# Local attention: half of a tile's columns shifted by one token, by two DMA transfers or by a shift matrix

## The reference, cut to what matters

```python
def shift_token(t):
    t1, t2 = jnp.split(t, 2, axis=-1)
    t2 = jnp.pad(t2, ((0, 0), (1, 0), (0, 0)))[:, :-1]
    return jnp.concatenate([t1, t2], axis=-1)

def _layer(x, wqkv, qs, ksc, wo, lg, lb, w1, b1, w2, b2):
    h = shift_token(x)
    ...                                   # q, k, v, rotary, attention in windows of 64 tokens
    x = x + o @ wo
    h = shift_token(x)
    mu = h.mean(-1, keepdims=True)
    var = h.var(-1, keepdims=True)
    h = (h - mu) / jnp.sqrt(var + 1e-05) * lg + lb
    h = h @ w1 + b1
    a, g = jnp.split(h, 2, axis=-1)
    h = a * jax.nn.gelu(g, approximate=False)
    x = x + h @ w2 + b2
```

## Time and profile before

| | |
|---|---|
| runs, not profiled: median (lowest, highest) | 1104.02 us (1098.06, 1105.16) |
| the profiled execution | 1102.0 us |
| its span, first to last instruction | 1100.2 us |
| mean granted TensorE clock | 0.899 of full speed |
| the four instances of `window_layer`, about | us 85 to 180, 192 to 290, 639 to 727, 743 to 838 |

### The profile page before, as it was taken

The page is one execution under the profiler, slowest core; times in us unless marked ns, Lnnn a source line. Parts: engine busy times, 40 slices in busy tenths (PEclk is TensorE's granted clock), DMA queues, the critical chain, the costliest instruction groups (busy, mean ns, idle before and its releaser), DMA issues.

```text
span 1100.2 us, 18999 instructions
## 1 busy us (share of the span) xinstructions
PE 881.5 (80%) x6776; PEld 536.6 (49%) x6776; DVE 665.9 (61%) x1736; ACT 491.6 (45%) x1010; POOL 468.4 (43%) x485
## 2 busy tenths in 40 slices
PE   6767998799836888999387679987988378889993
PEld 3544766377523444444245547754765234444442
DVE  5887885687576655311268688756875766543113
ACT  4114763676334653531041257636763346635310
POOL 4677871586411422200165778616864114222001
PEclk9998999999967896999789889899999669959997
DMA  9001100110000000000100011001100000000001
GB/s 364 31 2 30 26 16 1 30 26 17 1 0 1 1 1 1 1 1 1 39 2 1 1 30 26 16 1 30 26 16 1 0 1 1 1 1 1 1 1 38
DMA packets 11630, 21.62 MB, mean 20 GB/s; under 512 B 1424, under 2 KB 6928, under 8 KB 11024
## 3 DMA queue, kind: packets, MB, share of 16 engines
q1 hardware_dynamic: 11248, 18.60, 5.8%
q10 hardware_dynamic: 288, 1.78, 0.4%
HBM read 11.87 MB, written 1.05 MB: 12 GB/s over the span
## 4 chain that ended last, share of the span: by engine, by line
PE 48%; DVE 28%; POOL 9%; issue 6%; ACT 4%; DMA 1%; POOLq 1%; SPq 0%; DVEq 0%; ACTq 0%
PE bank L798 10%; PE bank L368 9%; PE bank L719 4%; DVE arena L1161 4%; PE bank L788 3%; PE bank L487 2%; DVE arena L859 2%; DVE arena L915 2%; DVE arena L1020 2%; PE bank L705 2%; PE bank L616 2%; POOL arena L1641 2%; PE bank L686 2%; POOL arena L1649 2%; PE bank L561 2%
## 5 line engine op out<-in xcount | busy, mean ns | idle before, releaser
L368 PE MATMUL bank<-consts_sb,arena 128*128 128x128 f32 x1024 | 160.5, 300 | 98.9 <-DVE arena L1153 26.2
L1290 ACT ACTIVATE arena<-bank 128x512 f32<-128x512 f32 (+2 forms) x300 | 146.4, 556 | 155.9 <-PE bank L368 93.6
L368 PEld LDWEIGHTS bank<-consts_sb,arena 128*128 128x128 f32 x1024 | 124.7, 152 | 170.0 <-issue 75.4
L1568 POOL TENSOR_TENSOR rstd<-vareps,neghalf 128x1 f32<-128x1 f32 x96 | 53.4, 558 | 254.5 <-DVE vareps L854 253.0
L1161 DVE TENSOR_REDUCE arena<-bank 128x2 f32<-128x1024 f32 (+3 forms) x128 | 98.1, 818 | 81.1 <-PE bank L673 80.5
L1697 POOL TENSOR_SCALAR_AFFINE_SELECT arena<-arena 128x256 f32<-128x256 f32 x128 | 51.3, 414 | 202.3 <-ACT arena L1481 199.4
L1641 POOL TENSOR_TENSOR arena<-arena,neghalf 128x16 f32<-128x16 f32 x32 | 93.1, 2908 | 66.0 <-DVE arena L1022 65.8
L487 PE MATMUL bank<-weights,x_features 128*128 128x512 f32 x192 | 102.1, 650 | 15.0 <-DVE arena L1035 9.2
L798 PE MATMUL bank<-arena,weights 128*128 128x512 f32 x256 | 111.9, 594 | 1.6 <-ACT arena L1537 1.6
L1481 ACT ACTIVATE arena<-bank 128x1024 f32<-128x1024 f32 (+1 forms) x96 | 81.5, 881 | 37.0 <-PE bank L705 36.6
L1408 ACT ACTIVATE arena<-bank,arena 128x128 f32<-128x128 f32 x256 | 69.7, 383 | 50.1 <-DVE arena L1063 50.1
(11 more groups left out here) (167 smaller groups left out, 1641.2 us busy)
## 6 DMA issues: line engine op xcount, KB each, us to landing
arena<-arena SPq DMA_DIRECT2D x56, 130.0 KB, 2.3
weights<-wts_dram SPq DMA_DIRECT2D x1, 2824.0 KB, 19.3
weights<-wts_dram SPq DMA_DIRECT2D x1, 1817.0 KB, 13.3
weights<-wts_dram SPq DMA_DIRECT2D x1, 1561.0 KB, 9.4
x_tokens<-x_dram SPq DMA_DIRECT2D x6, 256.0 KB, 3.2
consts_sb<-consts_dram ACTq DMA_DIRECT2D x1, 1226.5 KB, 7.2
out_dram<-x_inner SPq DMA_DIRECT2D x16, 64.0 KB, 1.5
consts_sb<-consts_dram SPq DMA_DIRECT2D x1, 768.0 KB, 4.7
```

The lines of the kernel that those rows point to most:

```text
L368: mm = pe.transpose(bank[:, i * P:(i + 1) * P], src, ident)
L1290: return act.activation(dst, src, ACT.Copy)
```

## The change

The shift of tile g is made by SP with two transfers inside SBUF: rows 0 to 126 of `xi[:, g, 64:128]` to rows 1 to 127 of `hn2`, and one row (the last token of the tile before, or zeros for the first tile of a sequence, taken from row 0 of the constant `carry`) to row 0. SP's loop gets G + 3 steps; after the value transfers of tile s it does `one_later(l, s - 3)`, which waits for xa_ready of tile s-3 and, from the third tile of all on, for PE's transpose of the tile two before it, since that used the same `hn2` buffer. DVE waits for hs_landed where it waited for pe_hs, and its copy and the wait for itself behind it are gone; its wait for pe_hT moves to `shifted_normed`. PE's two products, their PSUM bank use, the constant `shift` and POOL's wait for pe_hs are gone.

```diff
@@ window_layer, PE
-                    g = s - 4
-                    if 0 <= g < G:
-                        n = G * l + g
-                        pe.wait_ge(xa_ready, n + 1)
-                        bank = take(pe, ("hs", n), [(hs_kept, n + 1)], bank=BANK2["hs"])
-                        mm = pe.matmul(bank[:, 0:64], c_("shift"), xi[:, g, 64:P], start=True, stop=(g % NT == 0))
-                        if g % NT:
-                            mm = pe.matmul(bank[:, 0:64], c_("carry"), xi[:, g - 1, 64:P], start=False, stop=True)
-                        mm.then_inc(pe_hs, 1)
@@ window_layer, DVE
                 def shifted_stats(g):
                     n = G * l + g
-                    dve.wait_ge(pe_hs, n + 1)
+                    dve.wait_ge(hs_landed, 32 * (n + 1))
+                    dve.wait_ge(xa_ready, n + 1)
+                    norm_stats(first + g, [xi[:, g, 0:64], hn2[:, g % 2, 64:P]])
+
+                def shifted_normed(g):
+                    n = G * l + g
                     if n >= 2:
                         dve.wait_ge(pe_hT, hn_seen(n - 2))
-                    dve.tensor_copy(hn2[:, g % 2, 64:P], held(("hs", n))[:, 0:64]).then_inc(hs_kept, 1)
-                    dve.wait_ge(hs_kept, n + 1)
-                    dve.wait_ge(xa_ready, n + 1)
-                    norm_stats(first + g, [xi[:, g, 0:64], hn2[:, g % 2, 64:P]])
-
-                def shifted_normed(g):
                     norm_apply(first + g, hn2[:, g % 2, 0:64], xi[:, g, 0:64])
                     norm_apply(first + g, hn2[:, g % 2, 64:P], hn2[:, g % 2, 64:P]).then_inc(hn_ready, 1)
@@ gelu_layer, POOL
-                pool.wait_ge(pe_hs, G * (l + 1))
@@ SP
+            def one_later(l, g):
+                n = G * l + g
+                sp.wait_ge(xa_ready, n + 1)
+                if n >= 2:
+                    sp.wait_ge(pe_hT, hn_seen(n - 2))
+                ahead = xi[P - 1:P, g - 1, 64:P] if g % NT else c_("carry")[0:1, 0:64]
+                sp.dma_start(hn2[1:P, g % 2, 64:P], xi[0:P - 1, g, 64:P]).then_inc(hs_landed, 16)
+                sp.dma_start(hn2[0:1, g % 2, 64:P], ahead).then_inc(hs_landed, 16)
...
-                    for g in range(G):
+                    for s in range(G + 3):
+                        if s < G:
...
+                        if s >= 3:
+                            one_later(l, s - 3)
```

More of the change, by code:

```diff
@@ L57 @@
      ("rot2", NT * 4 * D2),
-     ("shift", 128), ("carry", 128)])
+     ("carry", 128)])
 MASKS_WIDTH = P
@@ L235, in build @@
          rot_ready, q_rotated, q_ready, pe_qT, pe_kT, qT_ready, kk_ready, vA_ready, pe_S, shift_ready, P_ready, pe_PT,
-         PT2_ready, pe_O, o_ready, pe_oT, oT_ready, pe_wo2, xa_ready, pe_hs, hs_kept, hn_ready, pe_wg, pe_wa, gel_ready,
+         PT2_ready, pe_O, o_ready, pe_oT, oT_ready, pe_wo2, xa_ready, hs_landed, hn_ready, pe_wg, pe_wa, gel_ready,
          hh_ready, xb2_ready, pe_w2, xf_ready) = (counter(n) for n in (
@@ L240, in build @@
              "pe_S", "shift_ready", "P_ready", "pe_PT", "PT2_ready", "pe_O", "o_ready", "pe_oT",
-             "oT_ready", "pe_wo2", "xa_ready", "pe_hs", "hs_kept", "hn_ready", "pe_wg", "pe_wa", "gel_ready", "hh_ready",
+             "oT_ready", "pe_wo2", "xa_ready", "hs_landed", "hn_ready", "pe_wg", "pe_wa", "gel_ready", "hh_ready",
              "xb2_ready", "pe_w2", "xf_ready"))
@@ L352, in build @@
         CENTRED1 = 6
-        BANK2 = {"hT": 3, "q": 0, "k": 1, "v": 2, "hs": 3, "qT": 4, "kT": 5, "oT": 3, "PT": (6, 2), "S": (4, 5),
+        BANK2 = {"hT": 3, "q": 0, "k": 1, "v": 2, "qT": 4, "kT": 5, "oT": 3, "PT": (6, 2), "S": (4, 5),
                  "wo2": 3, "O": (6, 2)}
@@ L993, in shifted_stats @@
                     n = G * l + g
-                    dve.wait_ge(pe_hs, n + 1)
-                    if n >= 2:
-                        dve.wait_ge(pe_hT, hn_seen(n - 2))
-                    dve.tensor_copy(hn2[:, g % 2, 64:P], held(("hs", n))[:, 0:64]).then_inc(hs_kept, 1)
-                    dve.wait_ge(hs_kept, n + 1)
+                    dve.wait_ge(hs_landed, 32 * (n + 1))
                     dve.wait_ge(xa_ready, n + 1)
@@ L1002, in shifted_normed @@
                 def shifted_normed(g):
+                    n = G * l + g
+                    if n >= 2:
+                        dve.wait_ge(pe_hT, hn_seen(n - 2))
                     norm_apply(first + g, hn2[:, g % 2, 0:64], xi[:, g, 0:64])
@@ L1748, in _ @@
                 for l in range(2):
-                    for g in range(G):
[L1750 to L1759, removed]
+                    for s in range(G + 3):
+                        if s < G:
+                            g = s
+                            n = G * l + g
+                            sp.wait_ge(vA_ready, n + 1)
+                            if n >= 4:
+                                sp.wait_ge(pe_O, 2 * (n - 3))
+                            sp.dma_start(vS2[64:P, n % 4, :, :], vA2[0:64, n % 4, :, :]).then_inc(vS_landed[n % 4], 16)
+                            if g % NT < NT - 1:
+                                if n >= 3:
+                                    sp.wait_ge(pe_O, 2 * (n - 2))
+                                sp.dma_start(vS2[0:64, (n + 1) % 4, :, :], vA2[64:P, n % 4, :, :])\
+                                    .then_inc(vS_landed[(n + 1) % 4], 16)
+                        if s >= 3:
+                            one_later(l, s - 3)
                 for g in range(G):
@@ L1864, in _layout @@
     later = np.where(i[None, :] > i[:, None], -1e30, 0.0)
-    c["shift"] = i[None, :] == i[:, None] + 1
     c["carry"] = (i[:, None] == P - 1) & (i[None, :] == 0)
```

## The result

The changed kernel takes 1133.76 us (median of six, 1132.91 to 1138.50), the kernel before, run beside it, 1102.3 us (1098.06 to 1105.16): a ratio of 1.0301 (95% interval 1.0279 to 1.0322). The forecast was 1158 in a range of 1108 to 1245, so sign and range hold, and the loss is 31.5 us instead of 56. The profiled execution spans 1132.4 us against 1100.2.

What follows compares the result with a forecast made beforehand. No engine has slack, so DVE's in-order wait for the shift closes a loop: 12.9 us in each of four instances, 52 us, plus 4 for the clock, on 1102.0 gives 1158 us, range 1108 to 1245.

Steps and rivals of the forecast that it cites:

- steps 1, 2 and 4 of the sum: DVE's shifted statistics start 2.0 us late, 8.0 by step 7 in a closed loop of 11.2 us steps, 12.9 after the drain.
- D(4): Start of DVE's shifted statistics in step 4, forecast 2.0 us late; the number in brackets is the step.
- L: Time from the shift's trigger until DVE may start its statistics: 5.0 us forecast, each us worth 28 us of time.
- One engine for 127 rows: 127 is prime, so one DMA engine carries the shift's rows, at 28.5 ns a packet; chance 0.70 at an ordinary pace.
- step 3: Step 8 of the kernel: PE's L627 ends an unchanged 17.66 us after step 7's statistics start; the next start is 11.8 late.
- step 6: Lower granted clock around the drain, some widening matmuls at the lower level: 1 us an instance, 4 us in all.
- xa(3): End of DVE's L1069 in step 3, making the rows that the next step shifts; the number in brackets is the step.
- (a) to (c): Removed: PE's L507 and L509, some 13 us; DVE's copy L997, 7 us at most; PE's wait for that copy, 7.3 us.
- (d): The drain's wait of DVE for the last shift, 2.33 us, is replaced, not removed.
- Sixteen engines: Rival: the shift's rows spread unevenly over sixteen engines, landing in 2.1 to 2.9 us, time about 1097 us; chance 0.12.
- Slow packets: Rival: one engine, but 60 ns per 256-byte packet, so a latency of 9.0 us and 1270 us; chance 0.10.
- The lower clock in the main steps: Rival: PE's gaps lower its clock, L627 becomes the trigger, steps of 12.5 us, 1180 us; chance 0.08.

Runs made afterwards that it cites:

- e5: Changed kernel with the 127-row transfer issued a second time into unused space and waited for too: 1195.7 us, ratio 1.0854 to the kernel before.
- e3: Changed kernel with DVE's shifted statistics moved later in steps 4 to 7, behind the maxima, transfers unchanged: 1113.3 us, ratio 1.0098 to the kernel before.
- e1: Changed kernel with one transfer of all 128 rows in place of 127 + 1, leaving out the shift: 1092.6 us, ratio 0.9913 to the kernel before.
- e8: Changed kernel with 128 unshifted rows, then a single row into unused space, both waited for: 1091.0 us in one execution.
- e2: Changed kernel with the 127 rows split into 112 + 15, so three transfers with the single row: 1107.6 us, ratio 1.0049 to the kernel before.
- e4: Changed kernel without transfer or wait for the shift, statistics and normalisation reading unshifted columns: 1087.2 us, ratio 0.9863 to the kernel before.

## Why the prediction was right, and where its sizes were off

**What bounds, and the closed loop (steps 1, 2 and 4 of the sum): right.** The first late moment is D(4), the main steps are DVE's 6.17 us plus L, the drain steps 1.15 plus L, in every instance. e5 gives 29 us per us of L where 28 were foreseen; e3 takes the cost away without touching the transfer, by moving what waits for it. The threshold was put at about L = 3.1, from steps of 9.2 us. Without PE's products and DVE's copy the steps are shorter: 8.99 us in e1 (D(5) = 237.70, D(8) = 264.67, no wait for the shift in them), and 8.99 - 6.17 gives about 2.8. That agrees with e1 and e8 (L 1.8 and 2.3: no loop) and with e2 (L 3.2 to 3.7: steps of 9.4 to 9.9).

**One engine for 127 rows: right.** e1, e8 and e2 show it. The Trainium skill ("DMA: Bandwidth & Descriptors", section on why a DMA increments its semaphore by 16 and not by 1) had given one engine for 127 partitions, and by that rule the traces agree, with shares of 0.08 against 0.77. What I had read from the trace before, that the transfers with equal shares each leave sixteen small packets, was a sound sign too, but my own test with it was wrong. The packets of the SP queue rose by 16368 - 11248 = 5120, and 5120 = 4096 + 1024 is what I had written down for sixteen engines. My count of packets for each transfer was off. The queue's rows of e1 and of e5:
```profile
q1 hardware_dynamic: 15856, 19.58, 6.2%
q1 hardware_dynamic: 20464, 20.62, 6.1%
```
e1 adds 4608 = 32 x (128 + 16) to the kernel before: an even transfer has sixteen end packets. e5 adds 4096 = 32 x (127 + 1) to the changed kernel: a transfer of 127 rows has one. The changed kernel's 160 a tile are then 127 + 1 for the 127 rows and 32 for the single row, which I had taken for one data packet. The sizes in the trace say the same: 4064 packets of 256 bytes, 512 of 16 bytes, and 544 = 32 x 17 ends of 4 bytes. So the single row goes as sixteen pieces of 16 bytes with sixteen ends, and the end packets do tell how many engines carry a transfer, if each transfer is counted by itself.

**The size of L: the term that was mis-sized.** I took 28.5 ns a packet from 512-byte packets to DRAM, so 3.6 us for 127, and 1.4 us for the rest. Measured: 14.1 ns and 1.8 us for the packets, 2.1 us for the rest, L = 3.93 and not 5.0. The packets cost half of what I took, nearer to the size scaled by bytes (17.6 ns, L = 3.6). The fixed part was too small by 0.8 us: it is 1.5 already in e1, the landing of the 127 rows is slower than that of an even transfer by 0.28 us and their start by 0.14, and the second transfer hides but for 0.18 us. These are two errors of opposite sign, 1.8 us too much and 0.8 too little; that they cancelled in part is luck. Read with L = 3.93, the prediction's slope takes 28 x 1.07 = 30 us off 1158 and leaves 1128, 6 us under the 1133.8 measured.

**The threshold on PE (step 3) and the clock (step 6): the first roughly right, the second too small.** In the second instance D(7) to the end of L618 in step 8 was to stay at 17.66 us. PE's timeline, steps 5 and 8 (counterpart of the earlier trace rows), and steps 8, 9 and 10 in the table of stretches (counterpart of the earlier trace rows):
```profile
256.05 0.33 PE L618 MATMUL bank<-consts_sb,arena 128*128 128x128 f32 x1
...
280.76 3.67 PE L368 MATMUL bank<-consts_sb,arena 128*128 128x128 f32 x16 [1.69 <-POOL arena L1644]
...
289.06 0.33 PE L618 MATMUL bank<-consts_sb,arena 128*128 128x128 f32 x1
```
```profile
280.00:291.00 11.00, 9.60 (x100) 8.16 (x101) 3.87 (x13) 5.53 (x14) 1.26 (x2) 0.70 0.01 2
293.30:298.30 5.00, 2.54 (x25) 2.08 (x20) 2.49 (x11) 1.88 (x2) 0.55 (x1) 0.85 0.05 10
298.30:303.30 5.00, 4.69 (x10) 2.14 (x10) 1.55 (x7) 0.69 (x1) 0.54 (x1) 0.50 0.03 7
```
289.39 - 270.65 = 18.7 us, 1.1 more, in a stretch whose granted clock is 0.70 (0.84 before). In step 10 it is 0.50, the lower level of 1.2 GHz throughout: PE had been busy for 2.5 of 5.0 us in step 9. From xa(3) to D(11) the four instances grew by 8.9, 6.3, 5.9 and 5.2 us, 26.3 together. The corrected sum gives 12.9 - 7 x 1.07 = 5.4 each, 21.6. The spans differ by 32.2, so 10.6 us are left, inside these stretches (4.7) and outside them (5.9), where I had written 4 for the clock. Of the 4.7, 3.5 lie in step 8: from D(7) to the end of L627 the kernel before takes 16.0, 17.7, 18.8 and 17.6 us in its four instances and the changed one to L618 18.7, 18.7, 18.6 and 17.6, so that the 17.66 us which I carried over is not a constant. That all of the 10.6 us is the clock and what follows from it is argued from these rows, not shown by an experiment.

**Who triggers: right, but barely.** The prediction left more than 1 us between PE's L627 and xa. In step 5 L618 ends at 256.38 and xa is 256.65: 0.3 us, and with the 0.7 us less of L in e2 L618 is the last in steps 5 and 7. SP waited last for DVE in 25 of 32 tiles of the changed kernel:
```profile
SPq L1725 <- DVE x_inner L1059: 46.0, 25, 5.4
```

**What the removed parts were worth.** (a) to (c) were put at 13, 7 and 7.3 us, all in the loop's shadow, and e4 shows 16 us for (a) to (d) together where no wait replaces them. (c) came back as the wait for L1071 in the waits of after.

**The rivals.** Sixteen engines: e1 and e8 show what it would have given, 1091 to 1093 us, where I had about 1097. Slow packets: fell, 14.1 ns and not 60. The rule of the Trainium skill ("DMA: Bandwidth & Descriptors", "Specifications"), that transfers under 512 bytes turn into a read-modify-write, is not seen here as a slow-down: 256 bytes every 14.1 ns are no slower by bytes than 512 in 28.5, though the second is busy time and not spacing, and the one kind goes inside SBUF and the other to DRAM. The lower clock in the main steps: fell, 1.00 there:
```profile
258.00:268.10 10.10, 8.89 (x103) 6.31 (x102) 8.79 (x22) 6.48 (x19) 8.05 (x7) 1.00 0.13 31
```

## What to carry to other kernels

Count the rows of a transfer that an in-order engine waits for: a shift by one leaves 127, which one DMA engine carries alone (1.8 us of packets against under 0.3 for 128), and 112 + 15 gave back 26 us of the 31.5. Then ask not how long it takes but what stands ahead of the wait: the same transfer was free in the main steps once DVE had other work first, and it stayed visible in the drain, where there is none. A cheap operation on a busy engine (here 0.4 us of PE and 0.2 of DVE a tile) may be better than a transfer of 2 to 4 us, unless its latency is covered.

## What the runs showed of the hardware that I had not expected

- Inside SBUF 128 or 112 rows have sixteen end packets, 15 rows have fifteen and 127 rows have one (in e2 the queue counts 17328 packets, 960 more than the changed kernel: 32 x (16 + 15 - 1)). A single row of 256 bytes goes as sixteen pieces of 16 bytes.
- Packets of 256 bytes follow each other every 14.1 ns on one engine, 18 GB/s.
- A second small transfer on a queue adds 0.5 us to the landing behind an even one (L 1.78 to 2.3) and 0.18 us behind 127 rows. These issues take 0.5 to 1.1 us of SP, and 1.7 to 2.0 us behind two with 127 packets for one engine.
- The last increment comes 0.35 us behind the last packet of an even transfer, and 0.62 us behind that of 127 rows.
